# Beta added in the first layer, four logits banks, an earlier branch test, and a re-ordered last group in a two-layer graph kernel

## The reference, cut to what matters

```
h = relu(layernorm(x));  x = x + quantised(adj @ quantised(relu(quant(h) @ quant(w))))
h = relu(layernorm(x));  R = (adj + I) / rowsum
Z = 0;  Xf = Xa = h
for s in 0, 1:
    logits = (Xa W1) W2 (Xa W3)^T;  A = softmax(logits cut to the smallest set with 90% of the row)
    Xf = R @ Xf;  Xa = A @ Xa;  Z = Z + Xf U1[s] + Xa U2[s]
out = x + layernorm(h + Z) * gamma + beta
```

## Time and profile before

| | us |
|---|---|
| three runs | 1308.89, 1310.68, 1313.84 |
| the profiled execution, its own time | 1313.01 |
| its span, to which all times of the trace refer | 1311.2 |
| busy: PE / DVE / ACT / POOL | 1116.9 / 1036.7 / 442.7 / 260.5 |
| granted TensorE clock, mean over the span | 0.942 of full |

### The profile page before, as it was taken

One profiled execution on the slowest core, in us unless ns is written; L12 is line 12 of the kernel. 1 busy time (PEld: TensorE's weight loads), 2 busy tenths in 40 slices (PEclk: granted clock), 3 DMA queues, 4 the chain that ended last, 5 costly groups with the idle time before them and its releaser, 6 DMA issues.

```text
span 1311.2 us, 16604 instructions
## 1 busy us (share of the span) xinstructions
PE 1116.9 (85%) x5402; PEld 515.1 (39%) x5402; DVE 1036.7 (79%) x2199; ACT 442.7 (34%) x836; POOL 260.5 (20%) x234
## 2 busy tenths in 40 slices
PE   0567999999999798899997998989995997898374
PEld 0223555554334344344443443334442443343131
DVE  7887777762798998888884019979989998998777
ACT  2544545455533134444331255631420521100000
POOL 6023323231312112012121113122110121111011
PEclk9888999999999899899998999999997999899786
DMA  6126656552424531533524433176633733733576
GB/s 235 63 83 214 234 184 223 171 188 72 140 85 147 127 74 41 105 73 65 138 57 96 82 113 118 60 256 178 136 104 86 166 89 99 174 95 100 172 210 203
DMA packets 190931, 172.19 MB, mean 131 GB/s; under 512 B 144704, under 2 KB 144704, under 8 KB 186752
## 3 DMA queue, kind: packets, MB, share of 16 engines
q1 hardware_dynamic: 190848, 171.23, 45.6%
HBM read 88.10 MB, written 49.55 MB: 105 GB/s over the span
## 4 chain that ended last, share of the span: by engine, by line
DVE 49%; PE 31%; issue 10%; ACT 4%; DMA 4%; SPq 1%; POOL 1%; DVEq 1%; POOLq 0%; ACTq 0%
DVE cand L1679 7%; DVE WS L1461 6%; PE UB L745 5%; DVE WS L1676 5%; DVE E L1692 5%; DVE WS L1684 4%; PE AB L735 3%; PE AB L728 3%; DVE g L1541 3%; PE RB L745 3%; PE RB L912 3%; DVE E L1691 3%; PE XB L745 2%; PE AB L912 2%; DVE cand L1719 2%
## 5 line engine op out<-in xcount | busy, mean ns | idle before, releaser
L1541 DVE TENSOR_REDUCE g<-E 128x1 f32<-128x2048 f32 x32 | 73.0, 2281 | 96.9 <-ACT E L1135 96.7
L1461 DVE SCALAR_TENSOR_TENSOR WS<-E,g 128x2048 bf16<-128x2048 f32 x48 | 120.5, 2553 | 0.4
L632 POOL TENSOR_TENSOR RT<-RT,AD 128x512 f32<-128x512 f32 x32 | 57.4, 1792 | 293.2 <-ACT RT L1194 293.1
L1679 DVE MAX8 cand<-WS 128x8 f32<-128x128 f32 x512 | 102.1, 277 | 1.1
L1135 ACT ACTIVATE E<-LB 128x512 f32<-128x512 f32 x128 | 75.4, 593 | 75.7 <-PE LB L835 60.4
L912 PE MATMUL AB<-VR,turns 128*128 128x512 f16 x256 | 67.0, 409 | 33.2 <-DMA turns<-E 33.2
L912 PE MATMUL RB<-VR,turns 128*128 128x512 f16 x256 | 64.1, 395 | 30.7 <-DMA turns<-E 30.7
L1684 DVE SCALAR_TENSOR_TENSOR WS<-E,g 128x2048 f32<-128x2048 f32 x33 | 81.1, 2456 | 0.9
L1171 ACT ACTIVATE E<-E,nmx 128x2048 f32<-128x2048 f32 x32 | 63.7, 1993 | 46.7 <-DVE nmx L1542 46.6
L912 PE MATMUL RB<-XR,turns 128*128 128x512 f16 x256 | 63.8, 394 | 17.8 <-DMA turns<-E 17.8
L1692 DVE SCALAR_TENSOR_TENSOR E<-WS,E 128x2048 f16<-128x2048 f32 x32 | 77.9, 2433 | 1.1
(11 more groups left out here) (307 smaller groups left out, 2174.5 us busy)
## 6 DMA issues: line engine op xcount, KB each, us to landing
turns<-adj_parts SPq DMA_DIRECT2D x48, 512.0 KB, 3.8
E<-adjT SPq DMA_DIRECT2D x16, 1024.0 KB, 7.6
adj_parts<-turns SPq DMA_DIRECT2D x16, 1024.0 KB, 5.2
AH<-adj_parts SPq DMA_DIRECT2D x16, 512.0 KB, 4.1
z_d<-UO SPq DMA_DIRECT2D x31, 256.0 KB, 2.3
XR<-x SPq DMA_DIRECT2D x4, 1024.0 KB, 11.8
WS<-U SPq DMA_DIRECT2D x4, 1024.0 KB, 7.7
x_d<-E SPq DMA_DIRECT2D x16, 256.0 KB, 2.0
```

The lines of the kernel that those rows point to most:

```text
L1461: return v.scalar_tensor_tensor(junk[t % 2], e, g4[:, k, t:t + 1], e, op, ALU.mult, accum_out=g4[:, F_, t:t + 1])
L1541: ct(v.tensor_reduce(row(A2)[:, t:t + 1], E[:, slot, :], AX.X, ALU.max))
L1679: i = v.max(cand[:, t, 8 * c:8 * c + 8], WS[:, c * PART:(c + 1) * PART])
```

## The change

- `order` (a ramp 1 to 2048 that the repair uses) gets a buffer of its own. gam moves to WF, bet to XHL, which are free when they are loaded.
- Beta is loaded at the start. POOL adds it to X1T in each tile of the first layer (`x1_beta`, between the root and the low half of XF) and writes X1B (in WF). SP stores X1B instead of X1T. DVE waits for POOL's add and not for the store.
- Logits go through LOGITS = LB0, LB1, TB0, TB1. A chunk waits for the chunk four back.
- In `settle`, the wait for the first mask moves from ahead of the flag's load and branch to behind them.
- At the end, the loads of tiles 0 to 7 wait no longer for s_kept = 2T but only for the transposes of earlier groups. Tiles 12 to 15 stay on chip in UO and XF (`ends`); their x1 is loaded into WS (`end_in`). DVE's order becomes batch 0, batch 1, tile 12, batch 2, tiles 13, 14, 15. Each is two fused operations per tile: (y - mean) * gamma while POOL takes the root, then y * root + x1.

```diff
         LB = [bank("LB0"), bank("LB1")]
         TB = [bank("TB0"), bank("TB1")]
+        LOGITS = LB + TB
...
             def l0_stores(t):
-                sp.wait_ge(s_x1, t + 1)
-                sp.dma_start(x1_d[t], X1T).then_inc(s_x1out, 16)
+                sp.wait_ge(s_x1b, t + 1)
+                sp.dma_start(x1_d[t], X1B[:, :]).then_inc(s_x1out, 16)
...
+            def fin_out(b, nth):
+                sp.wait_ge(s_res, nth)
+                if b:
+                    sp.wait_ge(s_out, 16 * b)
+                sp.dma_start(out[G * b:G * b + G].rearrange("t p d -> p t d"), fin_y[b % 2]).then_inc(s_out, 16)
+
+            def end_in():
+                sp.wait_ge(s_kept, 2 * T)
+                sp.dma_start(end_x, x1_d[T - G:T].rearrange("t p d -> p t d")).then_inc(s_endx, 16)
+
+            def end_out(t, nth):
+                sp.wait_ge(s_res, nth)
+                sp.dma_start(out[t], ends[t % 2][:, :]).then_inc(s_end[t % 2], 16)
...
                 if last:
-                    sp.wait_ge(s_kept, 2 * T)
-                    sp.dma_start(bet, beta.partition_broadcast(P)).then_inc(s_gb, 16)
-                    sp.dma_start(gam, gamma.partition_broadcast(P)).then_inc(s_gb, 16)
+                    sp.wait_ge(s_wl, T)
+                    sp.wait_ge(s_gb, 16)
+                    sp.dma_start(gam[:, :], gamma.partition_broadcast(P)).then_inc(s_gb, 16)
...
-                    if s and t < T - 1:
+                    if s and not last:
                         y_store(t)
+                    if last and i == 0:
+                        end_in()
+                        fin_out(0, 1)
                     if last and i == 1:
-                        fin_out(0)
                         fin_in(2)
-                        fin_out(1)
+                        fin_out(1, 2)
                     if last and i == 2:
-                        fin_in(3)
-                        fin_in(4)
+                        end_out(T - G, 3)
+                        fin_out(2, 4)
+                    if last and i == 3:
+                        end_out(T - G + 1, 5)
...
+            def x1_beta(t):
+                pool.wait_ge(s_x1, t + 1)
+                pool.wait_ge(s_x1out, 16 * t + OPEN)
+                q.tensor_tensor(X1B[:, :], X1T, bet, ALU.add).then_inc(s_x1b, 1)
...
             def l0_tile(t):
                 l0(t)
+                x1_beta(t)
                 x_lo(t, of(XR, t))
...
-                if gq or isinstance(t, int):
-                    pe.wait_ge(s_lc, m - 1 + OPEN)
-                elif c >= 2:
-                    pe.wait_ge(s_lc, NC * t + c - 1 + OPEN)
-                else:
-                    pe.wait_ge(s_lc, NC * t + OPEN)
+                pe.wait_ge(s_lc, (max(m - NC + 1, 0) if isinstance(t, int) else m - NC + 1) + OPEN)
...
-                    act.wait_ge(s_yout, 16 * t + OPEN)
-                    a(UO[:, :], bank[:, :], ACT.Copy, scale=rden[:, slot:slot + 1]).then_inc(s_ue, 1)
+                    act.wait_ge(s_yout, 16 * min(t, T - G) + OPEN)
+                    if t >= T - G + 2:
+                        act.wait_ge(s_end[t % 2], 16)
+                    y = ends[t % 2] if t >= T - G else UO
+                    a(y[:, :], bank[:, :], ACT.Copy, scale=rden[:, slot:slot + 1]).then_inc(s_ue, 1)
...
-                dve.wait_ge(s_x1out, 16 * t + OPEN)
+                dve.wait_ge(s_x1b, t)
...
-                ct(masked(tiles[0][0], 0, THR))
+                ct.free(masked(tiles[0][0], 0, THR))
+                first_kept = ct.base + ct.n
                 dve.wait_ge(s_const, 1)
                 dve.wait_ge(s_any, gq + 1)
                 any_flag = dve.value_load(total[0:1, 0:1].bitcast(I32))
...
+                dve.wait_ge(c_dve, first_kept)
                 for slot, t in tiles:
...
+            def normed(tiles, nth):
...
+                for k, (m, y, x1) in enumerate(tiles):
+                    (ch if k == n - 1 else ch.free)(v.scalar_tensor_tensor(y, y, mv[:, m, 0:1], gam[:, :], ALU.subtract,
+                                                                           ALU.mult))
+                dve.wait_ge(s_frs, nth)
+                for k, (m, y, x1) in enumerate(tiles):
+                    i = v.scalar_tensor_tensor(y, y, frs[:, m:m + 1], x1, ALU.mult, ALU.add)
+                i.then_inc(s_res, 1)
...
+            batch(0, 1)
+            batch(1, 2)
+            dve.wait_ge(s_endx, 16)
+            end(T - G, 3)
+            batch(2, 4)
+            for k in range(1, G):
+                end(T - G + k, 4 + k)
```

More of the change, by code:

```diff
@@ L179, in build @@
         ZT = Khl[:, 0, 0:2 * D].bitcast(F32)
-        FIN = [(G * b, G * b + G) for b in range(NG - 1)] + [(T - G, T - 1), (T - 1, T)]
+        BATCHES = NG - 1
         fin_y = [E[:, 2 * h, :].rearrange("p (t d) -> p t d", t=G) for h in range(2)]
@@ L186, in build @@
         mean_w = PKf
+        bet, X1B = XHL[:, :, :].rearrange("p h d -> p (h d)").bitcast(F32), WF
+        gam, ends = WF, (UO, XF)
+        end_x = WS[:, :].rearrange("p (t d) -> p t d", t=G)
         def halves_of(slot):
@@ L309, in _ @@
             u_in(0)
+            sp.dma_start(bet, beta.partition_broadcast(P)).then_inc(s_gb, 16)
             sp.dma_start(raw[:, 0, :], adjT[0]).then_inc(s_raw, 16)
@@ L665, in pairs @@
                         continue
+                    if g == NG - 1 and i == 0:
+                        root(0, 0, G)
+                    y = ends[t % 2] if g == NG - 1 else UO
                     pool.wait_ge(s_zin, 16 * t + 16)
                     pool.wait_ge(s_ue, t + 2 * T + 1 + OPEN)
[L668 removed]
+                    q.tensor_tensor(y[:, :], y[:, :], ZT, ALU.add).then_inc(s_y, 1)
                     if g == NG - 1:
[L671 to L674 removed]
+                        if i == 0:
+                            root(1, G, 2 * G)
+                        root(2 + i + (i > 0), t, t + 1)
+                        if i == 0:
+                            root(3, 2 * G, 3 * G)
             def last_post():
@@ new lines, in batch, with end @@
+            def batch(b, nth):
+                dve.wait_ge(s_finx[b % 2], 16 * (b // 2) + 16)
+                dve.wait_ge(s_finy[b % 2], 16 * (b // 2) + 16)
+                normed([(G * b + t, fin_y[b % 2][:, t, :], fin_x[b % 2][:, t, :]) for t in range(G)], nth)
+            def end(t, nth):
+                dve.wait_ge(s_y, t + 1 + OPEN)
+                normed([(t, ends[t % 2][:, :], end_x[:, t - (T - G), :])], nth)
+            dve.wait_ge(s_gb, 32)
+            batch(0, 1)
+            batch(1, 2)
```

90 lines of the change are left out of this document (32 added, 58 removed).

## The result

The changed kernel takes **1296.41 us** (median of 4 runs, 1295.24 to 1298.91) against 1311.91 for the kernel before in the same session (4 runs, 1308.89 to 1313.84). The ratio is 0.9886, with a 95% interval of 0.9861 to 0.9912: 1.1% faster, where I had said 1278.5 and 1269 to 1292. The direction is right, the size is half. The profiled execution took 1295.24 us, its span is 1293.3.

A forecast was written before the change was run, and what follows sets the result against it. No single engine was taken as the bound: PE leads the first layer and step 0, DVE step 1, SP's queue order the end. Savings of 3.5 + 7.0 + 0 + 21.7 = 32.2 us from 1310.7 gave 1278.5, range 1269 to 1292.

The forecast's parts named there:

- Four banks, 3.5: Step 0's logits loop: with four banks ACT copies faster and PE leaves sooner, 3.5 us saved (bounds 0 and 5).
- The wait in `settle`, 7.0: In step 1's groups the flag's load and branch run beside the mask: 7.0 us saved (0 to 9.5).
- Beta in the first layer, 0: POOL's 16 adds of beta in the first layer cost nothing: 0 us (bounds 0 and 8 us lost).
- rival 4: First layer: adds of up to 3.40 us hold up DVE, 2.6 us a tile over fourteen tiles, 1315; chance 0.03.
- The end, 21.7: After the last kept tile: earlier loads and reordered batches bring the last store from 1308.70 to 1287, 21.7 us saved.
- Rival 2: The end gives only about 12 us, through late waits in SP's queue or PE's low clock: 1288; chance 0.15.
- The wait that it put first: At the end, SP's wait for batch 0 ahead of tile 14's transposes can come late once the DMA queue is full.
- Rivals 1 and 3: 1: in `settle` the flag's load waits until DVE is empty, 1285, chance 0.15; 3: four banks do nothing, 1282, chance 0.08.
- still 13.34 us a tile: Sign for the first layer: if the adds of beta are free, a tile still takes 13.34 us.
- PE without a stop ahead of XB's transposes: Sign for the first layer: if the adds of beta are free, PE doesn't stop ahead of XB's transposes.
- over 65 us: Sign for the end: the prediction is wrong in its core if the end takes over 65 us; about 57 expected.
- The sum at the bounds: Whole kernel: with the parts at their bounds, the predicted time was said to be 1270 to 1287 us.

The follow-up runs named there:

- e7: The changed kernel with SP's loads of batch 2 moved ahead of the last of tile 14's four transposes; 1293.96 us, ratio 0.9867 to the kernel before.
- e6: The changed kernel with the wait for the mask put back ahead of the flag's load in `settle`; 1305.06 us, ratio 0.9951 to the kernel before.
- e5: The changed kernel with the logits' products back on two PSUM banks and PE's old waits; 1300.03 us, ratio 0.9912 to the kernel before.
- e4: The changed kernel with POOL's root of batch 2 moved behind the add of tile 13; 1290.83 us, ratio 0.9832 to the kernel before.

## Why the prediction was wrong

- **Four banks, 3.5.** Right: 3.6 in the stage, 3.0 when undone, and 3.6 in the median. The copies came at 0.57 us, my 0.58.
- **The wait in `settle`, 7.0.** Right: 6.8, and 6.2 when undone. The split differs from mine: the gap ahead of the first half shrinks by 3.2 us in the first group of step 1 (6.18 to 2.94), by 2.2 and 1.5 in the third and the last, and by 1.2 in the repaired one (6.6 to 5.4), 8.1 in all. In the last group 0.9 us of it is lost again: the four L1721 there take 10.1 us, where L1692 took 9.2, one of them 3.24 us beside a POOL add (L655); 0.6 come back, as that add stood beside L1691 before and made it 1.80 us instead of 1.23.
- **Beta in the first layer, 0. This step failed**, and it is the larger error. I had seen that DVE's normalisation could wait for the whole add, and by how much (0.93 measured, 1.27 in the prediction). I took as its cover the 2.2 us between ACT's K copies and PE's need of XB. But that is the cover of one consumer. The delay also goes round a loop of DVE and ACT that comes back to its own start in the next tile, and there 0.57 us were to spare. The row that told of it was in the trace of before: DVE's L1421 waited 0.27 us for PE in each of nine tiles in a row (179.69 to 286.41), in a loop I hadn't closed. The second part, SP's store of diag behind the later store of x1, I had dismissed because the adj tile is not needed for two tiles; L1436 needs the diag store in the next. Together 0.63 us a tile, and 9.0 us with the first tiles, outside my bound of 8. It is rival 4 in kind, at a quarter of its price and with adds of 1.27 us, not 3.40: I had put the point from which a delay costs at 2.2 us, and it is 0.57.
- **The end, 21.7. The second step that failed, by 5 us: the mechanism was right, the term too large.** Every link came in the order that I gave. Counted from SP's start (1220 predicted, 1218.78 measured), the loads of batch 2 came 3.6 us late, and this has three parts. PE started its second tile at 1237.37, where I had 1235.8 by that count: 1.6. The tile took 13.4 us and not 12.6: 0.8. And SP reached the loads 2.6 us behind the tile's end and not 1.4, since it was at the third of the four transposes and had the fourth to issue: 1.2. The landing of the loads took 9.2 us, not 8. The rest is less than 1 us each and goes both ways: DVE's statistics 3.1 us against 4, the root 1.5 against 1, PE's last tile 12.8 us against 12.4 (in the trace of before the two tiles after a pause took 12.7 and 13.2), and the tail. The last store came 5.0 us late. e7 gives 2.9 of this back; the split itself is read from the trace and no run tests it.
- **The rivals.** Rival 2 (the end gives about 12) named the right place and the right kind of cause, SP's order with the DMA queue full, at too high a price; the true 16.6 lie between it and the forecast. The wait that it put first, for DVE's batch 0, held SP for 0.9 us only (1239.44 to 1240.38). Rivals 1 and 3 are out by e6 and e5. The signs listed for the first layer ("still 13.34 us a tile", "PE without a stop ahead of XB's transposes") and for the end ("over 65 us") told the cases apart. The first failed: 13.97 us a tile, and the weight loads for XB's transposes now stop for 0.55 us. The second held with 62.4, though 57 was what I had expected.
- **The range** ended at 1292, 4.4 us below the result. The sum at the bounds, "1270 to 1287", doesn't follow from the bounds that I had stated: with the banks and `settle` at 0 and the first layer at its 8 us it is 1278.5 + 3.5 + 7.0 + 8 = 1297.0, with all at their best 1274.5, and the end, the largest term, had no bounds. A range up to 1297 would have held the result, but by luck: banks and `settle` came in as forecast, and it was the first layer, beyond its bound, and the end that failed.

## What to carry to other kernels

Before calling a delay on one engine covered, follow it round until it meets its own instruction in the next iteration: the cover is the least spare time of the loops it is in, not that of the consumer you thought of. Here a DVE instruction that waited a few tenths of a us for PE in each tile marked the loop. And price an operation on POOL by what DVE does in the same moment: here moving it by one place in its queue, beside the statistics, made it free.

## What the runs showed of the hardware

- A POOL instruction that starts just ahead of DVE's `tensor_scalar` of 128 x 512 fp32 holds it up, a fill that reads nothing too: 0.93, 0.39 and 0.17 us for POOL rows of 1.27, 0.725 and 0.524. There is no gap ahead of the DVE row; it is longer, and ends 0.28 us behind POOL's. The statistics beside an add took 0.69 us as always. Of two adds in a row DVE gets in between (1.48 and 1.37 us for two operations that take 0.55 and 0.43 alone). A DVE `scalar_tensor_tensor` of 128 x 2048 and an add that overlapped were both longer, 3.24 us against 2.29 and 1.70 against 1.27.
- The value load of the flag takes 0.31 us (0.56 in the first group of step 0) and runs in DVE's queue while the mask of 2.3 us runs on its datapath (1204.64 in the chain above); so does the branch. In the seven groups without a repair, DVE's idle time ahead of the first half is then 1.0 to 1.8 us in six and 2.9 in the first of step 1; before it was 3.2 to 6.2.
- Four transposes issued onto a quiet queue took SP 5.36 us, and 12.61 us behind 3 MB. So e4, which issues them 11.3 us sooner, shortens the end by 6.5 us only.
